# A four-layer convolution network on one core: one banded matrix per source row in the neighbour layer, in place of three diagonal ones

## The reference

```python
def _L1_conv_ref(x, gn_weight, gn_bias, w1, b1, w2, b2):
    counts = lax.stop_gradient(_df_counts(x))             # 1 to 8 neighbours for each pixel
    kvals = jnp.minimum(counts, K2).astype(jnp.int32).reshape(B, 1, P)
    patches = _unfold3x3_reflect(x).reshape(B, C, K2, P)  # the 9 pixels of the 3x3 window
    ...
    sim = jnp.einsum('bcp,bckp->bkp', cn, pn)             # cosine of the centre with each
    order = jnp.argsort(-sim, axis=1)
    top_sim = jnp.take_along_axis(sim, order, axis=1)
    mask = jnp.arange(K2)[None, :, None] < kvals
    wts = jnp.exp(top_sim) * mask
    wts = wts / jnp.sum(wts, axis=1, keepdims=True)
    pat_sorted = jnp.take_along_axis(patches, order[:, None, :, :], axis=2)
    out = jnp.einsum('bckp,bkp->bcp', pat_sorted, wts).reshape(B, C, H, W)
    enhanced = out + _group_norm(x, gn_weight, gn_bias)
    h = jax.nn.relu(jnp.einsum('oi,bihw->bohw', w1, enhanced) + b1[None, :, None, None])
    ffn = jnp.einsum('oi,bihw->bohw', w2, h) + b2[None, :, None, None]
    return enhanced + ffn
```

## Time and profile before

| | |
|---|---|
| time, median of 3 runs | 5995.22 us (5993.11 to 5998.76) |
| the profiled execution | 5991.41 us |
| its span in the profile | 5989.7 us |
| mean granted clock of TensorE | 0.91 |
| PE busy | 4923.8 us (82%) |
| DVE busy | 4262.5 us (71%) |
| POOL busy | 2947.9 us (49%) |
| ACT busy | 2608.8 us (44%) |
| DMA, 16 engines' share | q1: 15.0% |

### The profile page before, as it was taken

The page is one execution under the profiler, slowest core; times in us unless marked ns, Lnnn a source line. Parts: engine busy times, 40 slices in busy tenths (PEclk is TensorE's granted clock), DMA queues, the critical chain, the costliest instruction groups (busy, mean ns, idle before and its releaser), DMA issues. The chain is left out here.

```text
span 5989.7 us, 125121 instructions
## 1 busy us (share of the span) xinstructions
PE 4923.8 (82%) x46150; PEld 3813.6 (64%) x46150; DVE 4262.5 (71%) x7785; ACT 2608.8 (44%) x4832; POOL 2947.9 (49%) x2148
## 2 busy tenths in 40 slices
PE   2888888887878787816687687999979999999996
PEld 1656555555555555514454455777769999888885
DVE  5767677777777776768798748999955555666665
ACT  1656666666666665623343235666622111111110
POOL 1535353545454454533353337888843344444464
PEclk9989889898989898958898898999989999999998
DMA  3000000000000000033343220101030000000556
GB/s 144 16 30 16 30 16 30 16 30 16 30 16 30 16 27 19 9 107 105 103 144 123 79 82 21 52 36 49 35 144 0 0 0 0 0 0 0 39 42 144
DMA packets 359127, 268.73 MB, mean 45 GB/s; under 512 B 289440, under 2 KB 290720, under 8 KB 352544
## 3 DMA queue, kind: packets, MB, share of 16 engines
q1 hardware_dynamic: 355264, 258.30, 15.0%
q10 hardware_dynamic: 3424, 4.59, 0.2%
HBM read 156.27 MB, written 67.11 MB: 37 GB/s over the span
## 5 line engine op out<-in xcount | busy, mean ns | idle before, releaser
L527 POOL TENSOR_TENSOR l_probs<-l_probs,l_inv 128x1024 f32<-128x1024 f32 x256 | 492.5, 1928 | 568.5 <-DVE l_inv L937 567.9
L2388 ACT ACTIVATE l_both_hi<-l_both 128x256 fp32r<-128x256 f32 x252 | 106.6, 423 | 1253.5 <-DVE l_both L2494 1253.5
L1967 POOL TENSOR_TENSOR l_sum<-l_sum,l_prod 128x1024 f32<-128x1024 f32 x224 | 538.7, 2405 | 111.2 <-ACT l_prod L2064 92.7
L2147 DVE SCALAR_TENSOR_TENSOR l_acc<-l_xpad,l_w,l_acc 128x1024 f32<-128x1024 f32 x448 | 574.5, 1289 | 14.8 <-ACT l_acc L2048 1.3
L606 PEld LDWEIGHTS l_upper<-l_rows_T,l_hats 128*64 128x64 f32 x16384 | 516.4, 142 | 86.5 <-issue 84.7
L513 POOL TENSOR_TENSOR l_hats<-l_table,l_place 128x256 f32<-128x256 f32 x256 | 180.4, 705 | 764.7 <-PE l_upper L606 393.5
L773 ACT ACTIVATE l_probs<-l_probs,l_shift 128x256 f32<-128x256 f32 x1024 | 506.8, 496 | 103.2 <-DVE l_shift L922 101.4
L606 PE MATMUL l_upper<-l_rows_T,l_hats 128*64 128x64 f32 x16384 | 551.7, 227 | 0.0
L590 PE MATMUL l_lower<-l_hats,l_rpe 32*128 32x256 f32 x4096 | 315.6, 424 | 262.8 <-issue 119.9
L517 POOL TENSOR_TENSOR l_hats<-l_table,l_place 128x1024 f32<-128x1024 f32 x256 | 498.8, 1948 | 0.0
L898 DVE TENSOR_SCALAR l_hats<-l_hats 128x1280 f32<-128x1280 f32 x256 | 373.4, 1459 | 168.9 <-ACT l_hats L751 168.9
(11 more groups left out here) (316 smaller groups left out, 11884.0 us busy)
## 6 DMA issues: line engine op xcount, KB each, us to landing
l_xleft<-l_xt SPq DMA_DIRECT2D x64, 283.5 KB
l_xright<-l_xt SPq DMA_DIRECT2D x64, 283.5 KB
stat_xs<-in_x SPq DMA_DIRECT2D x8, 2048.0 KB, 23.1
l_hats<-in_x SPq DMA_DIRECT2D x8, 2048.0 KB, 7.8
l_xraw<-in_x SPq DMA_DIRECT2D x8, 2048.0 KB, 8.8
after_layer<-l_xraw SPq DMA_DIRECT2D x64, 256.0 KB, 2.0
l_xblk<-after_layer SPq DMA_DIRECT2D x32, 512.0 KB, 5.0
l_xsum<-after_layer SPq DMA_DIRECT2D x32, 512.0 KB, 5.5
```

The source lines that it names most:

```text
L527: pool.tensor_tensor(part, part, inv[:, u, cols].rearrange("c (j o) -> c j o", o=1).to_broadcast([C, 4, KEYS]), ALU.mult).then_inc(scaled_ ...
L1967: pool.tensor_tensor(part33(blk), part33(blk), rows(prod33[:, j % PRODUCTS, :]), ALU.add).then_inc(added33, 1)
L2147: last = dve.scalar_tensor_tensor(acc, src, tap, acc, op0=ALU.mult, op1=ALU.add)
```

## The change

For a source row and a target row, the three shifted diagonals are added up into one banded matrix, made by one multiplication: column x of the matrix has its three entries at rows x - 1, x and x + 1, and these rows have three different residues modulo 3. `band` is a constant of 64 x 66 with ones on three diagonals. `by_residue`, new, is run at the begin of each stage t >= 1 and sorts `wsrc` into `wres[row, source row, target row, r]`: for column residue r, the weight of the one shift that reaches this row, chosen by `residue`, a constant with three 0/1 columns. It takes nine DVE instructions over 3 x 66 elements, three of one input and six of two, in three groups, of which each waits for the one before. A build then multiplies `band` with three numbers repeated 22 times. The matrices are 66 columns wide, of which `gather` reads 64.

```diff
-        diag = mem.sbuf("diag", [C, 3, W])
-        wdiag = mem.sbuf("wdiag", [C, 9 * ROWS * W])
+        THIRDS = -(-W // 3)
+        BAND = 3 * THIRDS
+        band = mem.sbuf("band", [C, BAND])
+        residue = mem.sbuf("residue", [C, 3])
+        wres = mem.sbuf("wres", [C, H + 2, 3, 3])
+        wband = mem.sbuf("wband", [C, 3 * ROWS * BAND])
...
+                    for sign in (-1, 1):
+                        part = band[64 * b:64 * b + 64, :]
+                        chain.link(pool.affine_select(out=part, in_=part, compare_op=ALU.is_ge, fill=0.0, base=1,
+                                                      pattern=[[sign, BAND]], channel_multiplier=-sign))
                     for k in range(3):
-                        part = diag[64 * b:64 * b + 64, k, :]
-                        chain.link(pool.affine_select(out=part, in_=part, compare_op=ALU.not_equal, fill=1.0, base=-(k - 1),
-                                                      pattern=[[-1, W]], channel_multiplier=1))
+                        part = is_third[64 * b:64 * b + 64, k, :]
+                        chain.link(pool.affine_select(out=part, in_=part, compare_op=ALU.not_equal, fill=1.0, base=-k,
+                                                      pattern=[[-3, THIRDS]], channel_multiplier=1))
...
+                dve.reduce_sum(residue[:, :], is_third[:, :, :], axis=LX)
...
-                    for dx in range(3):
-                        for b in range(2):
-                            at = slice(64 * b, 64 * b + 64)
-                            last = pe.matmul(gather_ps[u][b][:, (s - 2 + first) * W:(s - 1 + final) * W], stage[at, u, s, :],
-                                             matrices(s)[at, dx, :, :].rearrange("p j x -> p (j x)"), start=False,
-                                             stop=(s == SOURCES - 1 and dx == 2))
+                    for b in range(2):
+                        at = slice(64 * b, 64 * b + 64)
+                        last = pe.matmul(gather_ps[u][b][:, (s - 2 + first) * W:(s - 1 + final) * W], stage[at, u, s, :],
+                                         matrices(s)[at, :, 0:W], start=False, stop=(s == SOURCES - 1))
...
-                    dve.tensor_tensor(matrices(s),
-                                      diag[:, :, :].rearrange("p d (o x) -> p d o x", o=1).to_broadcast([C, 3, n, W]),
-                                      wsrc[:, first:final + 1, :, bass.ds(c * ROWS + s, 1)].rearrange("p j d o -> p d j o")
-                                      .to_broadcast([C, 3, n, W]), ALU.mult).then_inc(diag_built, 1)
+                    dve.tensor_tensor(matrices(s).rearrange("p j (m r) -> p j m r", r=3),
+                                      band[:, :].rearrange("p (o m r) -> p o m r", o=1, r=3).to_broadcast([C, n, THIRDS, 3]),
+                                      wres[:, bass.ds(c * ROWS + s, 1), first:final + 1, :].rearrange("p o j r -> p j o r")
+                                      .to_broadcast([C, n, THIRDS, 3]), ALU.mult).then_inc(diag_built, 1)
+
+            def by_residue(t):
+
+                wait(dve, diag_built, (t - 1) * STEPS * SOURCES)
+                for k in range(3):
+                    for r in range(3):
+                        d = (k + 1 - r) % 3
+                        to = wres[:, :, :, r].rearrange("p y j -> p j y")
+                        if k == 0:
+                            last = dve.tensor_scalar(to, wsrc[:, :, d, :], residue[:, k:k + 1], None, ALU.mult)
+                        else:
+                            last = dve.scalar_tensor_tensor(to, wsrc[:, :, d, :], residue[:, k:k + 1], to, op0=ALU.mult, op1=ALU.add)
+                    link(last)
...
                 if t >= 1:
+                    by_residue(t)
                     scales(t)
```

More of the change, by code:

```diff
@@ L1094, in layer1 @@
             tmp = smem.sbuf("tmp", [C, B])
+            is_third = smem.sbuf("is_third", [C, 3, THIRDS])
             ps = smem.psum("ps")
@@ L1124, in _ @@
                 pool.memset(wsrc[:, :, :, :], 0.0)
-                chain.link(pool.memset(diag[:, :, :], 0.0))
+                pool.memset(band[:, :], 1.0)
+                chain.link(pool.memset(is_third[:, :, :], 0.0))
                 chain.link(pool.affine_select(out=mean8, in_=mean8, compare_op=ALU.is_ge, fill=0.0, base=0,
@@ L1252, in matrices @@
             widths = [targets(r)[1] + 1 - targets(r)[0] for r in range(SOURCES)]
-            start = sum(widths[:s]) * 3 * W
-            return wdiag[:, start:start + widths[s] * 3 * W].rearrange("p (d j x) -> p d j x", d=3, x=W)
+            start = sum(widths[:s]) * BAND
+            return wband[:, start:start + widths[s] * BAND].rearrange("p (j x) -> p j x", x=BAND)
         def apart(eng, at):
```

## The result

| | before | changed |
|---|---|---|
| time, median of 4 runs | 5994.16 us (5991.03 to 5998.76) | 5923.72 us (5918.35 to 5928.08) |
| ratio | | 0.9881, 95% interval 0.9864 to 0.9899 |
| the profiled execution, its span | 5991.41, 5989.7 us | 5918.35, 5916.6 us |
| PE, DVE busy | 4923.8, 4262.5 us | 4761.3, 4173.0 us |

It is faster, by 70 us, and by 1.2%. The forecast was 5885 us, a gain of 111; the time lies in the range given (5852 to 5940), in the slower half of it, and outside the forecast's own 5862 to 5915.

A forecast was written before the change was run, and what follows sets the result against it. PE was taken to bound stage 4, PE and DVE both nearly full in stages 1 to 3. Gather -45, stages 1 to 3 -80, sort +12.8, setup +1.5 gave -110.7 us, so 5885 us; range 5852 to 5940, the forecast's own 5862 to 5915.

The forecast's parts named there:

- a sign of being wrong: Layer 1, stage 2: a step over 18 us would show the forecast wrong; 16.8 us was expected.
- rival 1: Stages 1 to 3: DVE's short builds alternate with all four POOL instructions, step 19.9 us, time 5949 us; chance 0.13.
- The gather on PE: Layer 1: a third of the products remain, 5.6 us less a step; stage 4 gains 45 us, step 13.0.
- rival 3: Gather on PE: fixed part paid by each source row, stage 4's step 14.7 us, time 5910 us; chance 0.06.
- The builds: DVE in layer 1: a step's ten builds take 2.4 us instead of 5.5, 3.1 less.
- rival 4: Builds on DVE: rows of three cost 13 ns each, DVE's step 24.6 us, time 6042 us; chance 0.06.
- The sort: DVE, start of four stages: nine added instructions, 3.2 us each time, 12.8 us in all, bounds 10 and 21.
- DVE's step: Stages 1 to 3: 12.7 us of work plus 4.0 held up by POOL, 16.8 us; 80 us gained together.
- second chain: Stages 1 to 3: loop through the shifted copies over two steps, 33.1 us, so 16.6 us a step.
- rival 2: Stages 1 to 3: DVE held up less, PE with ACT sets a 15.6 us step, time 5860 us; chance 0.12.
- Rival 5: PE in layer 1: idling drops its clock to 1.2 GHz, steps double, time about 6260 us; chance 0.02.
- Setup's 1.5 us: Setup, once: ten mask selections on POOL instead of six, with the sum on DVE 1.5 us added.

## Why the prediction was right, and where it wasn't

The range held, but not because its account of stages 1 to 3 did. Their step of 18.85 us is over the 18 us that the prediction named as a sign of being wrong, and the range takes in the time because it reaches half way to rival 1, whose price isn't what was found. That part is luck.

- **The gather on PE: right.** Groups of 0.71, 1.25, 0.92 and 0.99 us against 0.72, 1.25, 0.93 and 1.03, step 12.96 us against 13.0. Stage 4, from the end of DVE's wait (3404.45 before, 3367.30 changed) to the end of the last stats, fell from 166.5 to 122.6 us; with 4.1 us of sort in it the shorter gather gave 48.1, forecast 45. Seven steps gave 5.7 each, as forecast, and the first 8.3. The fixed part is paid by group, so rival 3 falls. The last stats, before and changed:

```profile
3570.29 0.69 DVE L1659 BATCH_NORM_STATS2 all_stats<-l_res 128x6 f32<-128x512 f32 x1 [2.98 <-POOL l_res L1399]
...
3489.22 0.69 DVE L1681 BATCH_NORM_STATS2 all_stats<-l_res 128x6 f32<-128x512 f32 x1 [2.98 <-POOL l_res L1410]
```

- **The builds: right.** Ten in 2.42 us, forecast 2.4. All builds of the changed kernel by line (ns min/median/max, first and last start):

```profile
L1650 DVE TENSOR_TENSOR l_wband<-l_band,l_wres x320: 202/351/2514, 2752.2 to 3465.8; 128x198 f32<-128x198 f32 x96, 128x66 f32<-128x66 f32 x32, 128x132 f32<-128x132 f32 x32
```

  The median, 0.35 us, is that of 198 elements undisturbed: rows of three cost nothing extra where the result is written in one run, so rival 4 falls.
- **The sort: mis-sized.** Four times 4.15 us (2951.22 to 2955.37) is 16.6, forecast 12.8. The one-input instruction took 0.43 us and the two-input one 0.566, against 0.35 and 0.42 in the earlier trace rows, 1.2 and 1.35 times as long. Their results are written 36 bytes apart, as L880's are written with gaps, which only the bound used; that the gaps are the cause was not tried by itself.
- **Stages 1 to 3: the step that failed.** The stages' lengths fell by 10.0, 12.9 and 12.5 us; with the sort in each added back the steps gave 47.8, forecast 80. The prediction put it as "DVE's step: 12.7 + 4.0 = 16.8 us" and beside it a "second chain" that "gives nearly the same", 16.6, and took the larger. The terms of the first were right: over two steps DVE's own work is 25.1 us, forecast 25.4 (11.4 from the product at 3033.59 to the builds at 3044.99, and 1.16 for the builds, twice), and it is held up by 3.7 at the products, 3.7 and 0.9 at builds 0 to 4 and 0.3 at builds 7 to 9, 8.6 in all where 8.0 were forecast. But the wait for the copies (4.57) isn't another chain that runs beside these: 25.1 + 8.6 + 4.6 = 38.3, the time from 3013.39 to 3051.72. They are in series, since the copies start behind a turn that stands behind two gathers that wait for builds 0 to 4. The estimate of the second chain had only builds 5 to 9 and half the hold-up on it, 3.7 us over stage 0's 29.4; it was some 8 to 9. And the 29.4 has POOL's hold in it already: with POOL's products cut in the kernel before, the same two blocks of stage 0 take 27.1 us (2631.59 to 2658.65).
- **Layer 3: a term that the prediction didn't have.** The sum of layer 1 is 48.1 + 47.8 - 16.6 = 79.3 us, and its stage 1 begins 1.7 us earlier, but only 73.1 lie between the spans. From the end of layer 1's last stats to the end of the span the kernel before takes 2418.7 us and the changed one 2426.7. Late in layer 3's loop, whose code is the same, DVE waits longer for its own sums (before, changed):

```profile
5813.47 0.75 DVE L2504 SCALAR_TENSOR_TENSOR l_state<-l_sums_ps,l_state 128x256 f32 x1 [0.16 <-DVE l_sums_ps L2501]
...
5731.71 0.75 DVE L2527 SCALAR_TENSOR_TENSOR l_state<-l_sums_ps,l_state 128x256 f32 x1 [0.27 <-DVE l_sums_ps L2524]
```

  It isn't scatter: the runs with the old builds have 2419 to 2421 us behind layer 1, those with the new builds 2425 to 2428, except the two with the early sort, which have 2420. So it belongs to the program as a whole and not to banded matrices; the cause stays open.
- **The forecast's own step appears where the loop is opened:** with the turn first the mean is 17.1 us, against 16.8. And PE with ACT takes 15.3 us where POOL is small, the forecast's 15.1 and rival 2's 15.6.
- **Rival 1** had the right place, builds in a row each giving POOL a turn, and the wrong size: the hold is 4.3 us a step, near the forecast's 4.0 and not its 7.2. That 18.85 us lies between the forecast's 16.8 and its 19.9 comes from the wait for the copies. (The prediction calls this the mechanism of the second rival; it is the first's.) The Trainium skill, SBUF — State Buffer, section Who interferes with whom, has an exclusive hold between a VectorE instruction with two SBUF inputs and a GpSimd one that reads SBUF; that agrees with builds of 0.2 to 2.5 us on one line. The runs add that the hold matters only when it comes onto the chain that ends last.
- **Rival 5** was true in part: the clock fell to 0.90, not in stage 4 but where PE waits for builds. Ahead of the hidden product that took 3.78 us instead of 1.98 stand the two waits, 3.08 and 1.68 us; the granted clock is 0.51, the lower of the two levels, from 3033.6 to 3037.4 us, and 1.00 from 3010 to 3025 and from 3037.4 to 3047.8. The Trainium skill, TensorE: Matmul & The Clock Gate, section Part 1: The HAM clock gate, has an idle PE at half its clock; the trace agrees, with 0.51 behind those waits. What the clock alone costs on the loop, 1.8 us in every other step by these rows, was not tried by itself.
- **Setup's 1.5 us** can't be told apart from what else differs ahead of stage 1.

## What to carry to other kernels

Where two engines are nearly full at once, shortening both need not leave the larger of their new times: follow each engine's waits round the loop and ask what stands ahead of the instruction that feeds the next block, for waits that were hidden under the old bound can then add up. Many short two-input instructions on DVE beside POOL's long ones were dear here at their place in the order, not by their length. What starts the next block (here `gdiag` and the turn) belongs ahead of work that it doesn't need.

## What was not expected of the hardware

- The five old builds of source rows 0 to 4 took up to 8.89 us beside POOL's results and products, against 2.82; two new ones of 198 elements took 4.94 in the run with two queues.
- SP needs about 7 us to start a block's eight copies. Moving half of them to ACT's queue made single starts longer, brought the landing forward by about 0.7 us and the kernel by nothing.
- Two scalings of 0.48 us together, moved over one wait, gave 28 us with the turn first and 9 without.
- A layer whose code wasn't touched took 7 us longer or not, from one program to another.
